# Experts' gate and up as seven half-size products over 1,024 tokens, with down one stage late

## What is computed

```python
x = x + jnp.tanh(g_xattn[0]) * attention(_layernorm(x), ctx_1024, ...)

def _L0_ffn_ref(hidden_states, ...):             # of _layernorm(x)
    x = hidden_states.reshape(-1, D)
    scores = jax.nn.softmax(x @ router_w, axis=-1)
    topk_w, topk_idx = jax.lax.top_k(scores, TOP_K)      # 6 of 8
    g = jnp.einsum('td,edf->etf', x, w_gate)             # D=512, F=256
    u = jnp.einsum('td,edf->etf', x, w_up)
    f_all = jnp.einsum('etf,efd->ted', jax.nn.silu(g) * u, w_down)
    picked = jnp.take_along_axis(f_all, topk_idx[:, :, None], axis=1)
    y = jnp.sum(picked * topk_w[:, :, None], axis=1).reshape(B, S, D)
    return y + _glu_mlp(hidden_states, ws_gate, ws_up, ws_down)

x = x + jnp.tanh(g_ffn[0]) * _L0_ffn_ref(_layernorm(x), ...)
```

## Time and profile before

| | us |
|---|---|
| median of 3 runs | 2065.42 (2065.11 to 2065.54) |
| the profiled execution | 2062.74 |
| its span, first to last instruction | 2061.0 |
| TensorE busy | 2017.0 (98%) |
| VectorE busy | 1147.9 (56%) |
| ScalarE busy | 793.4 (38%) |
| GpSimd busy | 191.6 (9%) |

### The profile page before, as it was taken

The page is one execution under the profiler, slowest core; times in us unless marked ns, Lnnn a source line. Parts: engine busy times, 40 slices in busy tenths (PEclk is TensorE's granted clock), DMA queues, the critical chain, the costliest instruction groups (busy, mean ns, idle before and its releaser), DMA issues.

```text
span 2061.0 us, 32955 instructions
## 1 busy us (share of the span) xinstructions
PE 2017.0 (98%) x12160; PEld 1684.6 (82%) x12160; DVE 1147.9 (56%) x2766; ACT 793.4 (38%) x1974; POOL 191.6 (9%) x395
## 2 busy tenths in 40 slices
PE   6999999999997999999999999999999999999999
PEld 6899999999985778888888888777888888888887
DVE  6888888898887744333433343465334333333333
ACT  4777777777775522111111111243111111111111
POOL 3221221322212100000000000010000000000000
PEclk9999999999998999999999999999999999999999
DMA  7555655655643201000000010131001000100002
GB/s 210 136 132 139 149 128 143 148 129 144 142 104 126 82 21 31 21 21 21 31 20 20 20 31 21 62 103 41 21 21 31 21 21 20 31 31 20 10 1 82
DMA packets 117508, 138.36 MB, mean 67 GB/s; under 512 B 9728, under 2 KB 91648, under 8 KB 117376
## 3 DMA queue, kind: packets, MB, share of 16 engines
q1 hardware_dynamic: 117376, 136.63, 24.7%
HBM read 69.49 MB, written 16.78 MB: 42 GB/s over the span
## 4 chain that ended last, share of the span: by engine, by line
PE 63%; DMA 1%; DVE 1%; ACT 1%; POOL 1%; issue 1%; SPq 0%; POOLq 0%; DVEq 0%; ACTq 0%
PE gate_up L1181 41%; PE down L1200 21%; DMA acc<-x_between 1%; ACT xn L919 1%; DVE norm_stats L890 1%; DMA out<-acc 0%; PE gate_up L1158 0%; POOL norm_newton L97 0%; DVE xt_lo L1049 0%; PE down L1145 0%; PE gate_up L1165 0%; POOL norm_rstd L97 0%; ACT L1016 0%; POOL norm_newton L95 0%; DVE h L1088 0%
## 5 line engine op out<-in xcount | busy, mean ns | idle before, releaser
L1181 PE MATMUL gate_up<-xt_hi,e_hi 128*128 128x512 f32 x1280 | 507.3, 396 | 0.0
L1181 PE MATMUL gate_up<-xt_hi,e_lo 128*128 128x512 f32 x1280 | 506.4, 396 | 0.0
L1181 PE MATMUL gate_up<-xt_lo,e_hi 128*128 128x512 f32 x1280 | 506.3, 396 | 0.0
L1088 DVE TENSOR_TENSOR h<-gate_up,silu 128x512 f32<-128x512 f32 x160 | 110.5, 691 | 558.1 <-PE gate_up L1181 545.9
L1016 ACT ACTIVATE silu<-gate_up 128x512 f32<-128x512 f32 x160 | 95.7, 598 | 565.3 <-PE gate_up L1181 565.2
L1102 DVE SCALAR_TENSOR_TENSOR acc<-down,scale,acc 128x512 f32<-128x512 f32 x320 | 238.1, 748 | 109.3 <-PE down L1200 107.1
L1181 PEld LDWEIGHTS gate_up<-xt_lo,e_hi 128*128 128x128 f32 x1280 | 240.4, 188 | 58.3
L1181 PEld LDWEIGHTS gate_up<-xt_hi,e_hi 128*128 128x128 f32 x1280 | 240.5, 188 | 58.0
L1181 PEld LDWEIGHTS gate_up<-xt_hi,e_lo 128*128 128x128 f32 x1280 | 240.5, 188 | 57.6
L1019 ACT CAST h_hi<-h 128x512 fp32r<-128x512 f32 x160 | 99.4, 621 | 456.1 <-DVE h L1088 456.1
L1200 PE MATMUL down<-e_hi,h_hi 128*128 128x512 f32 x640 | 253.3, 396 | 0.9 <-DVE acc L1102 0.9
(11 more groups left out here) (129 smaller groups left out, 3300.6 us busy)
## 6 DMA issues: line engine op xcount, KB each, us to landing
k_stack<-k_hi SPq DMA_DIRECT2D x128, 128.0 KB, 2.6
q_stack<-q_hi SPq DMA_DIRECT2D x128, 128.0 KB, 2.6
w_raw<-in_w_gate SPq DMA_DIRECT2D x20, 512.0 KB, 3.7
w_raw<-in_w_up SPq DMA_DIRECT2D x20, 512.0 KB, 3.8
w_raw<-in_w_down SPq DMA_DIRECT2D x20, 512.0 KB, 3.6
c_in<-in_ctx_t SPq DMA_DIRECT2D x16, 512.0 KB, 3.6
x_in<-in_x SPq DMA_DIRECT2D x16, 512.0 KB, 3.8
k_stack<-k_lo SPq DMA_DIRECT2D x64, 128.0 KB, 2.6
```

Of the source, the lines that this page charges most:

```text
L1088: dve.tensor_tensor(h[f][:], gu_ps[f][:, 1, :], silu[f][:], ALU.mult).then_inc(h_made, 1)
L1181: ins = pe.matmul(gu_ps[f][:, which, :], (hi, lo)[a][:, c, f * P:(f + 1) * P], (xt_hi, xt_lo)[b][:, blk, c, :], start=(i == 0), stop=(i == ...
```

## The change

Gate and up of one expert are now computed for 1,024 tokens at once by a scheme of Strassen's kind (Winograd's form): the tokens are two halves of 512, the input width two halves of 256 (`CH`), the hidden width two of 128 (`FH`). Of each weight matrix there are 7 operands (two quarters as they are in A11, A12, one in A22, and four sums S1 to S4 that GpSimd makes, `weights_sums`), and of x there are 7 (B11, B21, B22 and T1 to T4, the sums again on GpSimd, `x_first`, `x_second`, `x_rest`). Seven products of 6 matmuls each go to four PSUM banks, in the order P1, P6, P2, P5, P7, P3, P4. P2 adds to P1's bank after ScalarE has copied P1 out (`copy_first`); P3 adds to P5's bank and P4 to P7's after VectorE has read them (`third_sum`, `sum_22`). VectorE makes five sums for each of gate and up (`second_sum`, `third_sum`, `sum_22`, `sum_12`, `sum_21`), and GpSimd multiplies three of the four blocks of silu(gate) with up (`gate_hidden`).

A stage is one expert over 1,024 tokens: 40 stages, all written out without a loop. TensorE's order in a stage is the products of gate, the products of up, and all of down of the stage before (8 tiles of 128 tokens, 48 matmuls, through a ring of four banks). The first of the ten stages of each 1,024 tokens (`opens`) has no down behind it; the last (`closes`) has its own down too, and after it the logits of the next 1,024 tokens. The routing of 1,024 tokens is done on VectorE in the opening stage. At the end of attention both first blocks of 512 tokens are prepared up to their normalising, and gate's and up's seven operands of the first expert are split. The logits' 16 rows are turned back by transposes in place of the matmuls with `fold`.

```diff
     def start_sync(sp):
-        load_x1(sp, 0)
+        sp.wait_ge(x1_stored, GROUPS * BLK // S * DMA)
+        for k in range(GROUPS):
+            load_rows(sp, k)
...
     def start_scalar(act):
-        for which in range(3):
-            split_hi(act, first_expert, which)
+        for k in range(GROUPS):
+            normalise(act, k)
+        weights_hi(act, 0, (W_A, W_C1, W_B))
+        weights_hi(act, 1, (W_A, W_C1, W_B))
...
     def start_vector(dve):
-        statistics(dve, 0)
-        for which in range(3):
-            split_lo(dve, first_expert, which)
+        for k in range(GROUPS):
+            statistics(dve, k)
+        for j in range(2):
+            for part in (W_A, W_C1, W_C2, W_B):
+                weights_lo(dve, j, part)
...
-        inverse_std(pool, 0)
+        for k in range(GROUPS):
+            inverse_std(pool, k)
+        for j in range(2):
+            weights_sums(pool, j)
...
+    PRODUCTS = ((A11, B11, ALPHA), (S2, T2, BETA), (A12, B21, ALPHA), (S1, T1, GAMMA),
+                (S3, T3, DELTA), (S4, B22, GAMMA), (A22, T4, DELTA))
+    P1, P6, P2, P5, P7, P3, P4 = range(1, 8)
...
+    def weights_hi(act, j, parts):
+        m, which = j // 2, j % 2
+        for part in parts:
+            if part == W_A:
+                act.wait_ge(raw_loaded[which], DMA * (m + 1))
+                wait(act, product_done, PARTS * (j - 1))
+                act.copy(ops_hi[:, which, W_PARTS[W_A]], w_source(which, W_A)).then_inc(ops_hi_made, 1)
+            elif part == W_C1:
+                act.wait_ge(w_sum_made, 4 * j + 4)
+                act.copy(ops_hi[:, which, S1:S4 + 1], w_sums[:]).then_inc(ops_hi_made, 1)
+            else:
+                act.copy(ops_hi[:, which, W_PARTS[W_B]], w_source(which, W_B)).then_inc(ops_hi_made, 1)
...
+    def weights_sums(pool, j):
+        which = j % 2
+        raw = raws[which]
+        a11, a12, a21, a22 = raw[:, :CH, :FH], raw[:, CH:, :FH], raw[:, :CH, FH:], raw[:, CH:, FH:]
+        pool.wait_ge(raw_loaded[which], DMA * (j // 2 + 1))
+        wait(pool, ops_lo_made, 4 * (j - 1) + W_C2 + 1)
+        pool.tensor_tensor(w_sums[:, 0], a21, a22, ALU.add).then_inc(w_sum_made, 1)
+        pool.tensor_tensor(w_sums[:, 2], a11, a21, ALU.subtract).then_inc(w_sum_made, 1)
+        pool.wait_ge(w_sum_made, 4 * j + 1)
+        pool.tensor_tensor(w_sums[:, 1], w_sums[:, 0], a11, ALU.subtract).then_inc(w_sum_made, 1)
+        pool.wait_ge(w_sum_made, 4 * j + 3)
+        pool.tensor_tensor(w_sums[:, 3], a12, w_sums[:, 1], ALU.subtract).then_inc(w_sum_made, 1)
...
+                def x_second(q):
+                    pool.wait_ge(xo_lo_made, PARTS * q + B11 + 1)
+                    pool.wait_ge(x_sum_made, 3 * q + 1)
+                    pool.tensor_tensor(x_half(X11), x_half(X22), t_sum[:], ALU.subtract).then_inc(x_sum_made, 1)
...
+                for m in range(STAGES):
...
+                    copy_first(2 * m)
+                    if not opens(m):
+                        hidden_hi(m - 1, C22)
+                        hidden_hi(m - 1, C12)
+                    down_hi(act, m)
+                    silu_first(m)
+                    silu(m, C22)
+                    silu(m, C12)
+                    if more:
+                        weights_hi(act, 2 * m + 2, (W_A,))
+                    silu(m, C21)
+                    if more:
+                        weights_hi(act, 2 * m + 2, (W_C1, W_B))
+                    if opens(m):
+                        exponentials(q)
+
+                    copy_first(2 * m + 1)
...
+                    if more:
+                        weights_hi(act, 2 * m + 3, (W_A, W_C1, W_B))
+                    hidden_hi(m, C11)
+                    hidden_hi(m, C21)
...
+                def route(q):
+                    mine, others = share[:].unsqueeze(3).to_broadcast(pairs_shape), share[:].unsqueeze(2).to_broadcast(pairs_shape)
...
+                    link(q, 9, dve.tensor_reduce(rank[:], ahead, AX.X, ALU.add))
+                    link(q, 10, dve.scalar_tensor_tensor(out=rank[:], in0=rank[:], scalar=TOP - 0.5, in1=share[:],
+                                                         op0=ALU.is_lt, op1=ALU.mult))
+                    link(q, 11, dve.tensor_scalar(scale[:, q, :, 0:E], rank[:], tanh_gates[:, 1:2], None, ALU.mult))
...
+                    second_sum(gate)
+                    if not opens(m):
+                        hidden_lo(m - 1, C22)
+                        hidden_lo(m - 1, C12)
+                    third_sum(gate)
+                    down_lo(dve, m)
+                    sum_22(gate)
+                    sum_12(gate)
+                    sum_21(gate)
+
+                    if opens(m):
+                        largest(q)
+                    if more:
+                        for part in (W_A, W_C1):
+                            weights_lo(dve, gate + 2, part)
+
+                    second_sum(up)
+                    if more:
+                        weights_lo(dve, gate + 2, W_C2)
+                        weights_lo(dve, gate + 2, W_B)
...
+                    hidden_first(m)
+                    third_sum(up)
+                    sum_22(up)
...
+                    if opens(m):
+                        route(q)
...
+                    sum_12(up)
+                    sum_21(up)
+
+                    if opens(m):
+                        hidden_lo(m, C11)
+                        hidden_lo(m, C21)
+                        for part in (W_A, W_C1, W_C2, W_B):
+                            weights_lo(dve, up + 2, part)
+                    elif not closes(m):
+                        for t, part in enumerate((W_A, W_C1, W_C2, W_B)):
+                            add(m - 1, t)
+                            weights_lo(dve, up + 2, part)
+                        add(m - 1, BT)
+                        hidden_lo(m, C11)
+                        add(m - 1, BT + 1)
+                        hidden_lo(m, C21)
+                        add(m - 1, BT + 2)
+                        add(m - 1, BT + 3)
...
+                def product(j, k):
...
+                    for c in range(CH):
+                        for i, (x, y) in enumerate(PASSES):
+                            ins = pe.matmul(gu_ps[bank][:], ops[x][:, which, a, c, :], xo[y][:, b, c, :],
+                                            start=(begins and c == 0 and i == 0), stop=(c == CH - 1 and i == len(PASSES) - 1), skip_group_check=True)
+                    ins.then_inc(product_done, 1)
...
+                    product(j, P1 - 1)
+
+                    pe.wait_ge(ops_lo_made, 4 * j + W_C1 + 1)
+                    wait(pe, sum_made, SUMS * (j - 1) + U2)
+                    if opening:
+                        pe.wait_ge(xo_lo_made, PARTS * q + T2 + 1)
+                    product(j, P6 - 1)
+
+                    pe.wait_ge(first_made, j + 1)
+                    product(j, P2 - 1)
...
+                    pe.wait_ge(sum_made, SUMS * j + V)
+                    product(j, P3 - 1)
+
+                    pe.wait_ge(ops_lo_made, 4 * j + W_B + 1)
+                    pe.wait_ge(sum_made, SUMS * j + SUM22)
+                    if opening:
+                        pe.wait_ge(xo_lo_made, PARTS * q + T4 + 1)
+                    product(j, P4 - 1)
...
-                def gate_up(n, f, logits_before=None):
...
-                        for c in range(C):
-                            for a, b in PASSES:
-                                ins = pe.matmul(gu_ps[f][:, which, :], (hi, lo)[a][:, c, f * P:(f + 1) * P],
-                                                (xt_hi, xt_lo)[b][:, blk, c, :], start=(i == 0), stop=(i == len(PASSES) * C - 1))
...
+                for m in range(STAGES):
...
+                    products(m, GATE)
+                    if opens(m):
+                        back(q)
+                    products(m, UP)
+                    if not opens(m):
+                        down(m - 1, 0)
+                        down(m - 1, 1)
+                    if closes(m):
+                        down(m, 0)
+                        down(m, 1)
+                        if n is not None:
+                            for g in range(GROUPS):
+                                logits(n, g)
...
```

788 lines of the change are left out of this document (470 added, 318 removed).

## The result

The changed kernel takes 2010.12 us in the median of four runs, the kernel before 2065.27; the ratio is 0.973, with a 95% interval from 0.972 to 0.975. The direction was forecast, but not the size: the time lies 48 us under the forecast of 2058 and 18 under the lower end of its range. The profiled execution took 2010.2 us, with a span of 2008.5 for 2061.0, so 52.5 us went where the sum has 7.

A forecast was written before the change was run, and what follows sets the result against it. TensorE, busy for 98% of the span, was taken as the bound. Start at 704.7, 1231.3 us of matmuls and small terms make 1972.9; waits of 80.9 give span 2053.8, forecast 2058 us, range 2028 to 2086.

The forecast's parts named there:

- The step of a matmul: Experts' part: matmuls of 512 columns follow each other at 0.2332 us, so 5,280 of them take 1231.3 us.
- The start: From attention's end to the experts: attention ends at 674.9, transposes start at 679.5, first product at 704.7; bounds 700 and 709.
- the 4.6 of the earlier trace: Between VectorE's last addition of attention and TensorE's first transpose of the experts: 4.6 us for the change of block.
- The turns of GpSimd and VectorE: Preparing x operands at the start: the two engines alternate, 1.2 and 2.4 us each, fourth operand ready at 699.6.
- Ordinary stages: 36 of 40 stages: up's third product waits 0.70 us for ScalarE's copy, gate 0.06 for VectorE; together 27.4 us.
- Openings: First stage of each 1,024 tokens: waits of 9.4 us plus 1.4 for clock, 10.8 x 4 = 43 us; bounds 6 and 15.
- the later waits (1.5 and 0.55): Behind each opening: the sixth and seventh products wait 1.5 and 0.55 us more, for VectorE's remaining work and GpSimd's sums.
- Closings: Three stages preparing the next tokens' operands: waits of 1.9, 0.9 and 0.7, 3.5 x 3 = 10.5 us; bounds 1 and 7.
- Small terms: Outside the products and down: 96 transposes 12.5 us, 60 logits matmuls 14.0, routing transposes 4.0, tail 3.4, seams 3.
- Rival B: GpSimd's and VectorE's turns fall kindly: start at 700, waits 54 us, span 2022.6, time 2027 us; chance 0.22.
- C: Gate in ordinary stages: late GpSimd holds VectorE's split of down, last product waits 0.73 us, 26 in all, 2084; chance 0.17.
- D: TensorE's clock drops to 1.2 GHz for 7 us at all seven changes of tokens: 19 us more, 2077 us; chance 0.11.

The follow-up runs named there:

- after_32: The changed kernel with 32 unused bytes ahead of xo_hi, so token operands and hidden tiles move and the weights stay: 2031.07 us, ratio 0.985 to the kernel before.
- comb: The changed kernel with four edits (ranking in the next stage, up's first copy earlier, start, closings) and the openings' exponential and shares later: 1951.30 us, ratio 0.945.

## Why the prediction was wrong

Its own steps, against the trace of after (TensorE's waits and steps as differences of starts):

- **The step of a matmul, the term that failed.** "5,280 x 0.2332 (1231.3)" measured 5,280 x 0.2267 = 1197.0: **34 us**. The prediction read a constant off one stretch of the kernel before and took it as a property of the matmul. It is one of the layout, which the diff replaces throughout, with unused tiles (`space0`, `space1`) in it; the prediction gives the step no bounds. The trace of before had the other value, 0.2271, in its attention part. What this term is worth as a run shows it is less: after_32, the changed kernel at the forecast's own step, takes 2031.07 us, which lies within the forecast's range. So the layout moves the time by 21 of the 48 us between forecast and result, and out of the range. The 34 belongs to a sum in which the slow matmuls behind waits are counted with the waits; the other 27 us of after_32 are the terms below.
- **Scheme and layout.** Which of the two gave the 55 us depends on the order in which they are taken. At equal remainders it is 2027.8 to 2010.1, 18 us for the scheme and 36 for the layout; with both kernels off it is 2063.7 to 2031.1, 33 us for the scheme and 21 for the layout.
- **The start.** First product at 698.4 for 704.7, by 6.3 less. Attention ends at 674.7 as forecast (674.9), but the transposes follow 0.85 us behind it and not 4.6, so the 4.6 of the earlier trace rows was not the price of a change of block; they start at 675.5 for 679.5. From there to the first product it is 22.9 us for 25.2. The turns of GpSimd and VectorE were assumed there for instructions that read two tensors from SBUF, with the earlier trace rows as a witness; its two VectorE rows, 1.35 and 1.39 us where the shortest of that line takes 0.54, are of a TENSOR_SCALAR, which reads one tensor. They fit taking turns, but are no witness for the condition.
- **Ordinary stages.** 0.94 us a stage for 0.76: the wait itself 0.59 for 0.70 and 0.05 for 0.06, and 0.30 in matmuls behind these waits that step at up to 0.236, which the sum did not have. 33.8 us for 27.4.
- **Openings.** 9.6 us for 10.8. The chain was right (5.39 for 5.95); the later waits (1.5 and 0.55) vanish but for one of 0.6 in the third, and half clock takes their place: 6.8 us at 1.2 GHz, of which 3.7 to 6.1 had matmuls in them, which cost 1.8 to 3.0 us for 1.4 forecast. 38.6 us for 43.
- **Closings.** 3.7 us for 3.5. Right in size and by the mechanism named, but the parts are not: 1.0 us for 1.9 at the rest of block 21, 1.6 for 0.9 behind it, 0.36 for 0.7. That the sum comes out is partly luck.
- **Small terms.** 96 transposes 9.9 for 12.5, the 60 logits' matmuls 13.9 for 14.0, the transposes for routing 2.8 for 4.0, the tail 3.5 for 3.4, seams nothing apart.

Sum: -34.3 for the step, -6.3 for the start, -4.7 for all the rest, which makes 2008.5 of 2053.8. **Rival B**, that vector engines' turns fall kindly, would have been credited with the low time by someone who looks at the result alone; the waits are 84 us and not 54. Its start at 700 did come (698.4), though 3.7 of the 6.3 us are the change of block. **C** did not come: gate's last product waits 0.05 us in an ordinary stage, as the forecast had it. **D** was half right: the clock fell at the four openings, for 6.8 us each, and at none of the closings.

## What to carry to other kernels

Take the step between back-to-back matmuls from the trace, but treat it as a property of the layout: when a change moves the operands' tiles, compute where they start (modulo 256 here) before and after. Here 32 unused bytes in the kernel before gave 36 us, and a scheme with 480 matmuls less gave 18 on top of them. A chain of queues is mended at the link that is late for no reason (the ranking in VectorE's queue), not at the one that the profile names as releaser (ScalarE's copy), and a contention between two engines moves along with the order unless the work is taken to where nobody waits.

## What the runs showed of the hardware that was not expected

- In the experts' part, matmuls of 512 columns with operands at the same remainder modulo 256 follow each other at 0.2267 us; at distances of 32, 64, 128 and 224 bytes at 0.230 to 0.233, at the same granted clock of 1.00 and with TensorE shown as busy all the time in both. In attention, where the remainders are equal too, such matmuls come in sixes and step at 0.226 to 0.233, as the followers of a late one do in the experts' part.
- With only one of three operands off by 32 bytes, all three matmuls of the group step slower (0.2295, 0.2316, 0.2340), and one that starts late behind a wait has some ten followers at 0.228 to 0.236 even with equal remainders. The cause behind this is open.
- The granted clock went to 1.2 GHz for 6.8 us at each wait of 5.2 in the changed kernel, falling before TensorE started again, and for 3.4 us at three of the four waits of 5.2 in after_32. It stayed at 2.4 GHz with waits of 1.6 and 1.1 us at the same place (comb).
